# A block of cross attention, quantised self attention and experts on one core: row maxima by a full-width matmul, output projection in 16-bit halves, an opening that loads half of the value weight and whole context columns first

## What is computed

```python
x = x + xattn(layernorm(x), ctx)      # 16 heads of 32; the change is here
x = x + self_attn(layernorm(x))       # 8-bit fake quantised
x = x + ffn(layernorm(x))             # 8 experts, top 2, capacity limited

def xattn(query, context):
    Q = (query @ Wq.T).reshape(B, T_q, 16, 32)
    K = (context @ Wk.T).reshape(B, T_c, 16, 32)
    V = (context @ Wv.T).reshape(B, T_c, 16, 32)
    scores = einsum('bqhd,bkhd->bhqk', Q, K) / sqrt(32)
    attn = softmax(scores, axis=-1)
    out = einsum('bhqk,bkhd->bqhd', attn, V).reshape(B, T_q, 512)
    return out @ Wo.T
```

## Time and profile before

| What | Value |
|---|---|
| Median of 3 runs | 1701.41 us |
| Profiled execution, its own time | 1701.77 us |
| Its span, first to last instruction | 1699.8 us |
| TensorE busy | 1617.4 us (95%) |
| VectorE busy | 1156.8 us (68%) |
| ScalarE busy | 767.6 us (45%) |
| GpSimd busy | 471.5 us (28%) |
| TensorE busy in 200 to 400 us | 199.91 of 200 us |
| Costliest line, VectorE L660 | 293.2 us, 128 instructions |
| Output projection L1027 | 25.6 us, 56 records |

### The profile page before, as it was taken

How to read it: one execution, slowest core, us unless ns; L and a number is a source line. 1 busy time by engine, 2 the same in 40 slices (tenths; PEclk the granted TensorE clock), 3 DMA queues, 4 the chain that set the end, 5 groups by cost and what they waited for, 6 DMA issues and landing times. The chain is left out here.

```text
span 1699.8 us, 39816 instructions
## 1 busy us (share of the span) xinstructions
PE 1617.4 (95%) x17264; PEld 1106.4 (65%) x17264; DVE 1156.8 (68%) x1400; ACT 767.6 (45%) x973; POOL 471.5 (28%) x412
## 2 busy tenths in 40 slices
PE   6999999999999999999999999887479999999998
PEld 4666666666666666666766666665257777777775
DVE  5678567568568657657756766567887676666766
ACT  5355336435345444445445435436445444444441
POOL 2323322232232123122213237532034411101133
PEclk9999999999999999999999999997789999999999
DMA  6444243253234234233232235350058556555544
GB/s 249 121 118 113 57 122 88 48 137 92 48 97 116 48 88 122 51 88 103 62 95 76 68 89 138 97 218 4 1 173 277 184 184 205 185 174 183 187 131 119
DMA packets 102151, 202.04 MB, mean 119 GB/s; under 512 B 25739, under 2 KB 25739, under 8 KB 101850
## 3 DMA queue, kind: packets, MB, share of 16 engines
q1 hardware_dynamic: 91258, 169.49, 34.5%
q0 software_dynamic: 10720, 30.02, 6.3%
HBM read 127.36 MB, written 18.90 MB: 86 GB/s over the span
## 5 line engine op out<-in xcount | busy, mean ns | idle before, releaser
L660 DVE TENSOR_REDUCE mx<-sc 128x4 f32<-128x2048 f32 x128 | 293.2, 2291 | 52.9 <-PE sc L906 52.1
L867 PE MATMUL proj<-w_hi,ctx 128*128 128x256 f16 x2048 | 268.6, 274 | 12.6 <-ACT ctx L445 12.5
L493 ACT ACTIVATE stage_w<-sc 128x1024 f32<-128x1024 f32 x256 | 248.2, 1025 | 70.4 <-PE sc L941 69.8
L881 PE MATMUL proj<-ctx,w_hi 128*128 128x512 f16 x1024 | 253.6, 380 | 0.0
L867 PEld LDWEIGHTS proj<-w_hi,ctx 128*128 128x128 f16 x2048 | 190.7, 98 | 62.2 <-issue 39.8
L456 ACT ACTIVATE stage_w<-proj 128x512 f32<-128x512 f32 x128 | 76.4, 597 | 320.8 <-PE proj L867 320.8
L389 POOL TENSOR_TENSOR acc_g<-stage_w 128x1024 f32<-128x1024 f32 x31 | 74.9, 2415 | 447.4 <-ACT stage_w L493 447.3
L682 DVE TENSOR_TENSOR acc_v<-acc_v,stage_w 128x1024 f32<-128x1024 f32 x93 | 116.1, 1248 | 87.2 <-ACT stage_w L493 84.4
L620 DVE SCALAR_TENSOR_TENSOR k_lo<-proj,k_hi 128x512 f16<-128x512 f32 x128 | 88.1, 688 | 122.7 <-ACT k_hi L465 121.9
L1172 DVE SCALAR_TENSOR_TENSOR w_lo<-stage_w,w_hi 128x2048 f16<-128x2048 f32 x64 | 144.8, 2292 | 34.3 <-ACT w_hi L1166 34.2
L881 PEld LDWEIGHTS proj<-ctx,w_hi 128*128 128x128 f16 x1024 | 90.0, 98 | 116.5 <-issue 25.1
(11 more groups left out here) (354 smaller groups left out, 2485.3 us busy)
## 6 DMA issues: line engine op xcount, KB each, us to landing
stage_w<-in_w SPq DMA_DIRECT2D x64, 1024.0 KB, 6.0
ctx_stage<-in_ctxT SPq DMA_DIRECT2D x64, 512.0 KB, 4.6
stage_w<-k_hi SPq DMA_DIRECT2D x256, 128.0 KB, 2.5
stage_w<-k_lo SPq DMA_DIRECT2D x128, 128.0 KB, 2.7
wq_f<-in_wiT POOLq DMA_DIRECT2D x24, 256.0 KB, 3.7
xg<-xbuf POOLq DMA_DIRECT2D x28, 176.0 KB, 4.5
obuf<-o_sb POOLq DMA_DIRECT2D x28, 176.0 KB, 3.5
xbuf<-final SPq DMA_DIRECT2D x17, 256.0 KB
```

The source lines that it names most:

```text
L493: act.activation(probs[:, u % 4, :], unit_scores(u), ACT.Exp, scale=1.0 / sqrt(HD)).then_inc(e_ready, 1)
L660: dve.tensor_reduce(mx[:, :, kb], sc[:, :, :], AX.X, ALU.max).then_inc(m_read, 1)
L867: last = pe.matmul(out, x_part[:, kb, e, col:col + P], w_part[:, 2, e, wv], start=term == 0 and e == 0, stop=term == 2 and e == EC - 1)
L881: last = pe.matmul(proj[at % 2][:, :], w_part[:, 1, e, P * (g % G):P * (g % G) + P], x_part[:, kb, e, :], start=term == 0 and e == 0, stop ...
```

## The change

Three parts. **Row maxima:** VectorE writes the negated maxima as four 16-bit columns 96 to 99 of a zeroed 128 x 128 matrix `nm_cols`; one matmul with the identity turns it, so that the maxima of head j stand in partition 96 + j of `misc`; ScalarE copies the four rows, each repeated for all four heads, and row 96 + j of `ks` is 1.0 for head j and 0.0 for the others (four GpSimd multiplications in the opening). The contraction has 100 rows in place of 97. **Output projection:** `wo` is loaded in float32 into `acc_v` and `acc_g` and split once into two halves; `finish_group` splits each `ot`, and the projection is 12 16-bit matmuls in place of 4 float32 ones. **Opening:** of the value weight only columns 0 to 255 are loaded first, the others behind `x[0]`, and the first two context pieces hold all four chunks of 256 columns.

```diff
-QKM = QK + 1
+QKM = QK + GH
-                load_w(0)
+                load_w(0, FIRST_COLS, w_in[0])
                 load_ctx(0, 0)
 ...
-                load_w(1)
+                load_w(1, ALL_COLS, w_in[1])
                 sp.dma_start(x1[:, 0, :], x[0]).then_inc(x0_in, 16)
-                load_w(2)
+                load_w(0, MORE_COLS, x0_in)
+                load_w(2, ALL_COLS, w_in[2])
 ...
-                sp.dma_start(wo[:, :, :], woT.rearrange("(c p) d -> p c d", p=P)).then_inc(wo_in, 16)
+                for n, half in enumerate((acc_v, acc_g)):
+                    sp.dma_start(half.rearrange("p (c d) -> p c d", c=2),
+                                 woT.rearrange("(c p) d -> p c d", p=P)[:, 2 * n:2 * n + 2, :]).then_inc(wo_in, 16)
 ...
                 gp.memset(ks[QK:P, :, :], 1.0).then_inc(rows_set, 1)
+                gp.wait_ge(rows_set, 1)
+                for j in range(GH):
+                    gp.tensor_scalar(ks[QK:P, j, :], ks[QK:P, j, :], ident[QK:P, QK + j:QK + j + 1], 0.0,
+                                     ALU.mult, ALU.add).then_inc(rows_set, 1)
 ...
                     act.activation(qs[QK:QKM, 4 * g:4 * g + 4, :],
-                                   misc[QK:QKM, :].rearrange("p (j t) -> p j t", j=GH), ACT.Copy).then_inc(row_set, 1)
+                                   misc[QK:QKM, 0:T].unsqueeze(1).to_broadcast([GH, GH, T]), ACT.Copy).then_inc(row_set, 1)
 ...
-                split_w(0)
+                split_w(0, FIRST_COLS)
 ...
                 split_xt(0)
+                split_w(0, MORE_COLS)
 ...
                 empty_bank(-1, LAST_V + 6)
+                act.wait_ge(wo_in, 32)
+                for n, half in enumerate((acc_v, acc_g)):
+                    act.activation(wo_hi[:, 2 * n:2 * n + 2, :], half.rearrange("p (c d) -> p c d", c=2), ACT.Copy,
+                                   scale=WSCALE).then_inc(w_hi_ready, 1)
                 split_q(0)
 ...
-                def maxima_to_diag(b, g, steps):
+                def negate_maxima(b, g):
                     dve.wait_ge(m_read, 16 * b + 4 * g + KB)
-                    steps.did(dve.tensor_reduce(nm[:, :], mx[:, :, :], AX.X, ALU.max, negate=True))
-                    steps.wait()
                     if not (isinstance(b, int) and b == 0 and g == 0):
                         dve.wait_ge(row_ready, 4 * b + g)
-                    dve.tensor_tensor(diag[:, :, :], nm[:, :].unsqueeze(2).to_broadcast([P, GH, T]),
-                                      ident16[:, :].unsqueeze(1).to_broadcast([P, GH, T]),
-                                      ALU.mult).then_inc(diag_ready, 1)
+                    dve.tensor_reduce(nm_cols[:, QK:QKM], mx[:, :, :], AX.X, ALU.max, negate=True).then_inc(nm_ready, 1)
 ...
                     steps.wait()
+                    dve.scalar_tensor_tensor(rden[:, :], po[:, 0:T], OSCALE, rden[:, :], ALU.mult, ALU.mult).then_inc(ot_ready, 1)
+                    dve.wait_ge(ot_ready, 4 * b + g + 1)
                     if g == 0 and not (isinstance(b, int) and b == 0):
                         dve.wait_ge(o_ready, b)
-                    dve.tensor_tensor(ot[:, g, :], po[:, 0:T], rden[:, :], ALU.mult).then_inc(ot_ready, 1)
+                    steps.did(dve.tensor_copy(ot_hi[:, g, :], rden[:, :]))
+                    steps.wait()
+                    dve.tensor_tensor(ot_lo[:, g, :], rden[:, :], ot_hi[:, g, :], ALU.subtract).then_inc(ot_split, 1)
 ...
-                dve.wait_ge(x0_in, 16)
+                dve.wait_ge(x0_in, 32)
 ...
-                    pe.matmul(misc[QK:QKM, :], ones16[:, 0:1], diag[:, :, :].rearrange("p j t -> p (j t)"),
-                              start=True, stop=True, tile_position=(0, QK)).then_inc(row_ready, 1)
+                    pe.matmul(misc[:, 0:T], nm_cols[:, :], ident16[:, :], start=True, stop=True).then_inc(row_ready, 1)
 ...
-                    pe.wait_ge(ot_ready, 4 * b + 4)
+                    pe.wait_ge(ot_split, 4 * b + 4)
                     pe.wait_ge(row_set, 4 * b + 5)
-                    for g in range(G):
-                        last = pe.matmul(misc[:, :], ot[:, g, :], wo[:, g, :], start=g == 0, stop=g == G - 1)
-                    last.then_inc(o_ready, 1)
+                    project_heads(pe, misc[:, :], wo, ot).then_inc(o_ready, 1)
 ...
-                pe.wait_ge(rows_set, 1)
-                pe.wait_ge(wo_in, 16)
+                pe.wait_ge(rows_set, 1 + GH)
+                pe.wait_ge(w_lo_ready, 6)
 ...
+def project_heads(pe, bank, wo, ot):
+    wo_hi, wo_lo, ot_hi, ot_lo = out_views(wo, ot)
+    n_mm = 0
+    for o_part, w_part in mm_terms(ot_hi, ot_lo, wo_hi, wo_lo):
+        for g in range(G):
+            last = pe.matmul(bank, o_part[:, g, :], w_part[:, g, :], start=n_mm == 0, stop=n_mm == 3 * G - 1)
+            n_mm += 1
+    return last
```

More of the change, by code:

```diff
@@ L163, in cross_attention @@
         wo_in = sem("wo_in")
+        ot_split = sem("ot_split")
         w_in = [sem(f"w_in{i}") for i in range(3)]
@@ L715, in _ @@
                     split_k(0, 0, kb)
+                    if kb == 0:
+                        split_w(0, MORE_COLS, 4)
+                for n, half in enumerate((acc_v, acc_g)):
+                    dve.wait_ge(w_hi_ready, 4 + n + 1)
+                    dve.scalar_tensor_tensor(wo_lo[:, 2 * n:2 * n + 2, :], half.rearrange("p (c d) -> p c d", c=2), WSCALE,
+                                             wo_hi[:, 2 * n:2 * n + 2, :], ALU.mult, ALU.subtract).then_inc(w_lo_ready, 1)
                 split_q(0)
@@ L1599, in _ @@
                 transpose_xn(3)
-                for g in range(G):
-                    last = pe.matmul(pb[:, 0, :], ot[:, g, :], wo[:, g, :], start=g == 0, stop=g == G - 1)
-                last.then_inc(vx_ready, 1)
+                project_heads(pe, pb[:, 0, :], wo, ot).then_inc(vx_ready, 1)
                 for n, (c, j) in enumerate(BANKS):
```

81 lines of the change are left out of this document (49 added, 32 removed).

## The result

The changed kernel takes 1682.66 us (median of 4 runs, 1681.23 to 1687.38) against 1701.51 us before (median of 4, one more run than above): a ratio of 0.989, 95% interval 0.9867 to 0.9912. The forecast was 1688.5 us, 5.8 us too slow, and the measured time lies 0.16 us inside the fast end of the range. The profiled execution took 1682.83 us, its span 1681.0. On the forecast's own scale (1701.77 to 1682.83) the gain is 18.9 us where 12.9 were worked out.

A forecast was written before the change was run, and what follows sets the result against it. TensorE was taken to bound the cross attention, transfers and engine chains the opening. Row maxima -9.6, last group -0.9, projection -6.4 and opening +4.0 sum to -12.9 us: 1688.5 us on the median's scale, range 1682.5 to 1695.0.

The forecast's parts named there:

- rival 1: Opening: it costs nothing, as VectorE's splits pass between GpSimd's multiplications; 1684.5 us, or 1684.0; chance 0.22.
- first scores near 44.5 us: Opening: sign that the forecast is right, first scores for the maxima starting there in place of 40.49 us.
- Rival 4: Opening transfers: 1 KB rows are slower, 0.17 us a row or more to decide; about 1719.5 us; chance 0.02.
- Row maxima, TensorE: Cross attention groups: shorter full-width row matmul saves 0.33 us a group, batch 0's four counted half; 9.6 us.
- Rival 2: Row matmul: the loss around it stays, coming from the wait, not the shape; 4.9 less, 1693.4 us; chance 0.13.
- Last group: Last cross attention group: `diag` (0.7) and the shorter matmul (0.2) leave the chain of waits; 0.9 us saved.
- Projection: Output projection: 0.88 us saved in each of seven batches, 0.3 in the last after VectorE's 0.58; 6.4 us.
- rival 3: Last group stays at full clock, about 3 us less, 1685.5 us; opposite, self attention slowed, 1691.5; chance 0.11 both ways.
- Opening, the step that failed: Opening: GpSimd's multiplications alternate with VectorE's splits, key weight's split 3.6 us later; with clock loss 4.0 us lost.
- Opening, what it brings: Opening: TensorE may start near 9.5 in place of 12.47 us, but nothing counted; at most 0.5 us gained.
- 1 KB rows: Opening transfers: 1 KB rows for 2 MB in place of 2 KB; cost taken as 0, +5.4 at equal time per row.
- Extra clock stretch in the opening: Opening: TensorE idles some 3 us twice and may run the next matmuls at 1.2 GHz; 0.6 us lost.

The follow-up runs named there:

- e5: Changed kernel with the row-maxima matmul writing only partitions 96 to 127, as a 32-column stationary at array position 96: 1694.07 us, one run.
- e6: Kernel before with its row of maxima made by a full-width matmul, ones repeated for 128 partitions, 512 moving columns kept: 1698.2 us, one run.
- e2: Kernel before with only the output projection changed to 12 16-bit matmuls: 1698.75 us, ratio 0.9972.
- e1: Kernel before with only the new row maxima, including GpSimd's four early multiplications: 1692.19 us, ratio 0.9928.
- e7: Changed kernel with the load order of before in the opening, multiplications still early: 1687.8 us, ratio 0.9905.
- e4: Changed kernel with GpSimd's four multiplications moved behind its transfers of the first queries: 1683.3 us, ratio 0.9885.
- e9: The changed kernel, unaltered, run a second time: 1682.78 us, ratio 0.9887 against the kernel before.
- e8: Changed kernel with the opening's order rewritten on ScalarE, VectorE and TensorE (V copies before `std`) and GpSimd's multiplications late: 1680.39 us, ratio 0.9876.
- e3: Kernel before with only the opening by columns changed, no multiplications: 1701.6 us, ratio 0.9991.

## Why the prediction was off, step by step

The time came out 5.8 us under the forecast, nearest to rival 1 (1684.5 us, chance 0.22), and it is luck that it still lies in the range, by 0.16 us: the range reached down to the rivals, while the opening's term of the sum was wrong. Of the signs given, first scores near 44.5 us failed (41.10), but so did rival 1's, 40 or before. Rival 4 falls: from 10 us on the transfers ran at 375 to 388 GB/s.

- **Row maxima, TensorE: right.** 0.33 us was worked out, 0.34 is in the row and 0.36 a group in the trace. Rival 2 is refuted by e5 and e6. I counted batch 0's groups half because TensorE waits for maxima there; they paid in full (1.12 us over three). Both together are 10.9 us up to the last group but one in place of 9.6 with all groups: 1.3 us.
- **Last group: right in size** (0.99 us, 0.9 forecast), by the wait that fell from 1.11 to 0.39 us and the shorter matmul.
- **Projection: right for the seven** (0.88 us each, 0.90 in e2). At the end the two terms were right as well: the projection gave 0.84 us, and VectorE's two new instructions took 0.6 us (the wait of 1.68 us that became 2.34), where 0.88 and 0.58 were forecast. Yet from the last group's row matmul to the experts 1.48 us were gained, where 0.3 were forecast. 1.0 of the difference lies between the last row matmul and the wait, where the new rows alone bring it too (e1), and the half clock there, 3.4 us shorter, fits it: rival 3, at a third of its 3 us. The other 0.2 us lie behind the projection, where profiles differ by up to 3.5 us, and are chance as far as these runs tell.
- **Opening, the step that failed.** "They would alternate ... the key weight's split ends at 24.5 in place of 20.94, 3.6 us later": it ended at 21.36. The mechanism is real: 1.6 to 1.7 us for each split that began inside a multiplication, and 2.8 us at the key weight's split in e1 and e7, where splits stand back to back. (The row that I read it from says a little less than I wrote: L614 ended at 139.43 us, 1.08 and not 1.2 us behind GpSimd's end at 138.35.) But (1) I charged each of four multiplications to VectorE, while GpSimd waited as often, up to 4.94 us for one; (2) with the opening by columns VectorE had gaps between its splits (2.35 us ahead of the key weight's in e4), which took up most of what was left: what the multiplications cost at the key weight's split is 0.43 us here and 0.87 in e9 (3.16 us for 2.29); (3) of the 0.9 us by which piece 4 and the copy of V1 started late (22.96 and 23.92 in place of 22.09 and 23.04) only 0.5 reached the first key block (27.83 in place of 27.36). The term of 4.0 us is 0.6 in the profile and about zero over three profiles of each opening. What holds TensorE in the new opening is the order on ScalarE, which the forecast named: V3 waits for the copy of V1 whether the multiplications are early or late (2.60 us in both), and e8, which changes that order, is 4.7 us earlier.
- **Opening, what it brings: right, for a part.** Nothing was counted, and e3 shows nothing (0.9991). But beside the early multiplications it is worth about 2 us in the profiles (first scores at 43.00 and 43.49 in e1 and e7, at 41.03 in the mean with it): two parts that I priced each by itself, and one hides the other. The times lean the same way without showing it (0.9905 in e7, 0.989 and 0.9887 with it; the intervals overlap).
- **1 KB rows: not quite zero.** The last part of piece 4 landed at 22.94 us in place of 21.41, and ScalarE waited 0.36 us for it; in e9 and e4, with the same rows, it landed at 21.96 and 22.05. A packet of 1 KB took 46 ns (median) and one of 2 KB 86, so a KB costs 7% more, and from 5 to 10 us the rate was 300 GB/s in place of 363. That can be part of the 0.6 us, and is far from rival 4's 0.17 us a row.
- **Extra clock stretch in the opening:** absent in the first profile of the changed kernel, present in its second (e9) and in e3, e4 and e5 (3.4 us long each). In e3 and e4 it came behind the wait of 2.6 us for the copy of V1, as the 0.6 us of the sum had it, and the later first scores (42.02 and 41.53) fit it; e9's stretch began at 19.0 us and cost less, since TensorE waits right behind it, then 0.94 us, for the copy of V1 in any case.

In us: opening 3.4, groups 1.3, end 1.2, and 0.1 of small terms make the 6.0 between 12.9 and 18.9. What stays open is the stretch between the cross attention and the experts: why its half clock lasts 3.4 us in one execution and 6.8 in another was not tried.

## What to carry to other kernels

When two engines hold each other up, do not charge every overlap to the one you care about: read which of them waits, and how much gap it has behind it. Price a new instruction together with the order of the work it meets, since an order that looks worthless alone may be what hides it. And look at several profiles of an opening, or of a stretch with pauses of TensorE, before believing a microsecond there.

## What the runs showed of the hardware

- A matmul on a corner of the array (1 or 32 stationary columns at position 96) between full-width ones cost about 0.2 us beside its columns at both lengths tried: 0.25 against 0.05 us for 128 columns (e5, changed kernel), 0.39 against 0.21 for 512 (before, e6).
- Two-input splits of VectorE and a 32 x 2048 16-bit multiplication on GpSimd held each other up in both directions: the multiplication took 1.98 us alone and up to 4.94 beside splits (changed kernel), a split of 2.29 us became 3.97 (e1, e7).
- Three openings of the same code differed by 1.75 us in when the first scores start (40.12 to 41.87 us), with half clock at different times.
- The same stretch between the cross attention and the experts took from 135.7 to 139.2 us in fourteen profiles, behind the last edit of any of them.
